# One queue per slot parity in the weight staging, one semaphore per staging slot, and matmuls that wait for layer-norm chunks one by one

## What is computed

```python
def layer(x, W_r, W_i, lambd, W_fc, ln_w, ln_b, W_proj):      # x: 16 x 2048 x 1024
    u = layernorm(x)                                          # over the 1024 features
    r = sigmoid(u @ W_r.T); i = sigmoid(u @ W_i.T)
    log_a = 8.0 * r * log_sigmoid(lambd)
    a = exp(log_a); b = sqrt(max(1 - exp(2 * log_a), 0)) * (i * u)
    h[t] = a[t] * h[t-1] + b[t]                               # scan over time
    x = x + h
    v = gelu(layernorm(x) @ ternary(W_fc).T)                  # 4096 features
    return x + layernorm(v, ln_w, ln_b) @ ternary(W_proj).T
# ternary(W): sign(W) * min(round(|W| / mean|W|), 1)
```

## Time and profile before

| what | us |
|---|---|
| timed runs, two | 2238.38 and 2451.46 |
| their median | 2344.92 |
| the profiled execution, its own time | 2241.78 |
| its span on core 2, the slowest | 2240.2 |
| spans of the other cores | 2213.9 to 2233.6 |
| PE busy, of the span | 1478.6 (66%) |
| DVE busy | 1017.4 (45%) |
| ACT busy | 619.1 (28%) |
| POOL busy | 312.0 (14%) |

### The profile page before, as it was taken

How to read it: one execution, slowest core, us unless ns; L and a number is a source line. 1 busy time by engine, 2 the same in 40 slices (tenths; PEclk the granted TensorE clock), 3 DMA queues, 4 the chain that set the end, 5 groups by cost and what they waited for, 6 DMA issues and landing times.

```text
span 2240.2 us, 20128 instructions; the slowest of 8 cores (2213.9 to 2240.2 us)
## 1 busy us (share of the span) xinstructions
PE 1478.6 (66%) x6052; PEld 610.7 (27%) x6052; DVE 1017.4 (45%) x1457; ACT 619.1 (28%) x1013; POOL 312.0 (14%) x308
## 2 busy tenths in 40 slices
PE   0045104765868867795959595959497777858697
PEld 0012001221323323341424142423242333323243
DVE  0144655663553255425642565145623553256413
ACT  0038332110432234122423132214221332224220
POOL 0122122531120021101110111011100110011100
PEclk9978556986888979796969697979797888979799
DMA  4546797852312122211320231113021312122114
GB/s 123 140 150 230 220 295 235 192 142 75 106 45 104 48 72 79 103 48 38 113 103 10 66 122 38 66 47 123 29 104 47 95 57 104 48 66 85 66 31 129
DMA packets 103745, 223.67 MB, mean 100 GB/s; under 512 B 34516, under 2 KB 34516, under 8 KB 103640
## 3 DMA queue, kind: packets, MB, share of 16 engines
q1 hardware_dynamic: 91352, 178.34, 25.4%
q0 software_dynamic: 12288, 44.05, 6.8%
HBM read 192.98 MB, written 29.37 MB: 99 GB/s over the span
## 4 chain that ended last, share of the span: by engine, by line
PE 58%; DVE 17%; DMA 12%; issue 6%; ACT 6%; DVEq 0%; POOL 0%; SPq 0%; ACTq 0%; POOLq 0%
PE pY L498 21%; PE pool L782 19%; PE pool L631 5%; PE pool L642 3%; PE pS L768 2%; DMA xb<-wit 2%; PE pQ L770 2%; DVE tmp L601 2%; DVE ln_bf L603 2%; DVE tmp L283 2%; DMA xb<-wfct 2%; DVE ln_bf L285 2%; PE pS L472 2%; DMA wp_sc<-qn_buf 2%; DMA t_i<-wpt 2%
## 5 line engine op out<-in xcount | busy, mean ns | idle before, releaser
L782 PE MATMUL pool<-ln_bf,wfc_q 128*128 128x512 bf16 x2048 | 506.8, 394 | 100.3 <-DVE ln_bf L285 100.3
L498 PE MATMUL pY<-g_sb,wp_sl 128*128 128x512 bf16 x2048 | 467.5, 389 | 57.4 <-DVE tmp L520 41.1
L782 PEld LDWEIGHTS pool<-ln_bf,wfc_q 128*128 128x128 bf16 x2048 | 206.0, 101 | 371.2 <-issue 146.8
L498 PEld LDWEIGHTS pY<-g_sb,wp_sl 128*128 128x128 bf16 x2048 | 203.7, 100 | 314.7 <-issue 85.1
L790 ACT ACTIVATE g_sb<-pool 128x512 bf16<-128x512 f32 x256 | 152.6, 597 | 445.0 <-PE pool L782 444.9
L797 DVE TENSOR_TENSOR gsq<-g_sb 128x512 bf16<-128x512 bf16 x224 | 95.4, 426 | 389.9 <-ACT g_sb L790 377.5
L631 PE MATMUL pool<-ln_bf,wr_sl 128*128 128x512 bf16 x512 | 141.2, 425 | 113.8 <-DVE ln_bf L603 113.8
L666 ACT ACTIVATE t_r<-pool 128x512 f32<-128x512 f32 x64 | 37.9, 592 | 374.7 <-PE pool L631 374.7
L601 POOL TENSOR_TENSOR t_r<-xb,rs_t 128x512 f32<-128x512 f32 x16 | 25.6, 1600 | 760.7 <-DVE mb_t L482 759.6
L642 PE MATMUL pool<-ln_bf,wi_sl 128*128 128x512 bf16 x512 | 125.8, 390 | 0.0
L689 DVE SCALAR_TENSOR_TENSOR t_q<-t_a 128x512 f32<-128x512 f32 x64 | 44.2, 691 | 176.6 <-ACT t_a L677 176.6
(11 more groups left out here) (119 smaller groups left out, 1677.2 us busy)
## 6 DMA issues: line engine op xcount, KB each, us to landing
wp_sl<-wp_sc SPq DMA_DIRECT2D x128, 512.0 KB, 4.1
xb<-x SPq DMA_DIRECT2D x8, 2048.0 KB, 9.1
wr_sl<-wr_sc SPq DMA_DIRECT2D x64, 256.0 KB, 2.7
wi_sl<-wi_sc SPq DMA_DIRECT2D x64, 256.0 KB, 2.9
xb<-wfct SPq DMA_DIRECT2D x32, 512.0 KB, 7.0
xb<-wfct POOLq DMA_DIRECT2D x32, 512.0 KB, 6.9
y<-xb SPq DMA_DIRECT2D x8, 2048.0 KB, 7.8
t_q<-wpt POOLq DMA_DIRECT2D x16, 512.0 KB, 5.3
```

Of the source, the lines that this page charges most:

```text
L498: fn = lambda E, kh=kh, sl=sl, bank=bank, first=(kh == 0), last=last: E.matmul(pY[bank][:, :], wp_sl[:, sl * 2048 + (kh % 16) * 128: sl * ...
L782: fn = lambda E, h=h, d=d, bank=bank: E.matmul(pool[bank][:, :], wfc_q[:, d * H + h * 128: d * H + h * 128 + 128], lnch(d), start=(d == 0) ...
```

## The change

Four things are changed. Line numbers of the new code are not given; names are the same.

1. Staging: all eight pieces of W_r come first, then those of W_i, and the slot of `qn_buf` now has the parity of `kd`. So load and scatter of a piece stand on the same queue. The loads of the rearranged slices wait for the last scatter of each of the four slots.
2. The pass over both big weights: `iload` is gone, each piece's two loads stand in the piece's own turn, and the W_proj load counts on the semaphore of the W_fc load of its slot (`d_stg0` to `d_stg3`).
3. The second pass over W_proj uses the same four semaphores; `d_stg4` and `d_stg5` no longer exist.
4. Products with `ln_bf` (both gates and FC1) take the chunks in the order `DPERM`, each with a wait for its own chunk. Line 708 on VectorE waits for chunk `e` alone.

```diff
+DPERM = (0, 1, 6, 2, 3, 7, 4, 5)
...
-    tok_wsc = {}
-    for kd in range(ND):
-        for widx, (WSRC, WSC) in enumerate(((WRT, wr_sc), (WIT, wi_sc))):
-            slot = (kd * 2 + widx) % 4
+    for widx, (WSRC, WSC) in enumerate(((WRT, wr_sc), (WIT, wi_sc))):
+        for kd in range(ND):
+            slot = (widx * ND + kd) % 4
...
-            tok_wsc[(widx, kd)] = emit_scatter(slot, dst, src2)
+            emit_scatter(slot, dst, src2)
+    tok_wrsc = list(sc_last.values())
+    tok_wisc = []
...
-        iload(0)
-        iload(1)
         for i in range(32):
...
-            iload(i + 2)
-            tl = fcq_tl.pop(i)
-            tl2 = gp_tl.pop(i)
+            usewait(qeng, ("stg", sl))
+            tl = b.emit(qeng, lambda E, st=st, kd=kd, pc=pc:
+                        E.dma_start(st, WFCT[128 * kd:128 * (kd + 1), 1024 * pc:1024 * (pc + 1)]),
+                        inc=f"d_stg{sl}", n=16)
...
+            tl2 = b.emit(qeng2, lambda E, st2=st2, i=i:
+                         E.dma_start(st2, WPT[128 * i:128 * (i + 1), :]), inc=f"d_stg{sl}", n=16)
...
-                              E.dma_start(st, WPT[128 * i:128 * (i + 1), :]), inc=f"d_stg{4 + sl % 2}", n=16)
+                              E.dma_start(st, WPT[128 * i:128 * (i + 1), :]), inc=f"d_stg{sl}", n=16)
...
-            b.wait("tensor", tok_ln1)
-            b.wait("tensor", tok_ln1g)
...
-            for d in range(ND):
-                fn = lambda E, d=d, sl=sl, pR=pR: E.matmul(
+            for ii, d in enumerate(DPERM):
+                b.wait("tensor", ln1lt[d])
+                fn = lambda E, d=d, sl=sl, pR=pR, ii=ii: E.matmul(
                     pR[:, :], wr_sl[:, sl * D + d * 128: sl * D + d * 128 + 128], lnch(d),
-                    start=(d == 0), stop=(d == ND - 1))
+                    start=(ii == 0), stop=(ii == ND - 1))
...
-            b.wait("vector", tok_ln1)
-            b.wait("vector", tok_ln1g)
+            b.wait("vector", ln1lt[e])
...
-        b.wait("tensor", tok_ln2[0])
-        b.wait("tensor", tok_ln2[1])
...
-            for d in range(ND):
-                fn = lambda E, h=h, d=d, bank=bank: E.matmul(
+            for ii, d in enumerate(DPERM):
+                b.wait("tensor", tok_ln2[d])
+                fn = lambda E, h=h, d=d, bank=bank, ii=ii: E.matmul(
```

More of the change, by code:

```diff
@@ L323, in emit_prep2a_mid @@
             st = xstg[sl]
-            st2 = tstg[sl]
-            iload(i + 2)
-            tl = fcq_tl.pop(i)
-            tl2 = gp_tl.pop(i)
+            qeng = "sync" if sl % 2 == 0 else "gpsimd"
+            usewait(qeng, ("stg", sl))
+            tl = b.emit(qeng, lambda E, st=st, kd=kd, pc=pc:
+                        E.dma_start(st, WFCT[128 * kd:128 * (kd + 1), 1024 * pc:1024 * (pc + 1)]),
+                        inc=f"d_stg{sl}", n=16)
+            st2 = tstg[sl]
+            qeng2 = "sync" if sl % 2 == 0 else "gpsimd"
+            if i < 4:
+                usewait(qeng2, (tkeymap[sl], 0))
+                usewait(qeng2, (tkeymap[sl], 1))
+            else:
+                usewait(qeng2, ("tstg", sl))
+            tl2 = b.emit(qeng2, lambda E, st2=st2, i=i:
+                         E.dma_start(st2, WPT[128 * i:128 * (i + 1), :]), inc=f"d_stg{sl}", n=16)
             b.wait("vector", tl)
@@ L355, in emit_prep2a_mid @@
         tok_x[1] = b.emit("sync", lambda E, d=dst1, s=src1: E.dma_start(d, s), inc="d_x1", n=16)
-        return (ln2_toks[5], ln2_toks[7])
+        return [ln2_toks[c] for c in range(ND)]
     p2b_loads = {}
@@ L531, in emit_wri_load @@
         usewait("sync", ("wrsl", sl))
-        for kd2 in range(ND):
-            b.wait("sync", tok_wsc[(0, kd2)])
+        for t_ in tok_wrsc:
+            b.wait("sync", t_)
         tok_wr[(k, e, 0)] = b.emit("sync", lambda E, e=e, sl=sl:
@@ L536, in emit_wri_load @@
         usewait("sync", ("wisl", sl))
-        for kd2 in range(ND):
-            b.wait("sync", tok_wsc[(1, kd2)])
+        for t_ in tok_wisc:
+            b.wait("sync", t_)
         tok_wr[(k, e, 1)] = b.emit("sync", lambda E, e=e, sl=sl:
@@ L591, in emit_ln1 @@
         pr = tok_ln2_of.get(k - 1)
-        tok_bc1 = rows_and_bcast(tstat1, 2, rs_t, mb_t, prev_read=pr[0] if pr else None,
-                                 prev_read_g=pr[1] if pr else None)
+        tok_bc1 = rows_and_bcast(tstat1, 2, rs_t, mb_t, prev_read=pr[5] if pr else None,
+                                 prev_read_g=pr[7] if pr else None)
         lt = []
@@ L605, in emit_ln1 @@
             lt.append(tln)
-        tok_ln1_of[k] = (lt[5], lt[7])
+        tok_ln1_of[k] = lt
         free.pop(("lnbf",), None)
@@ L613, in build_nc @@
         seq, t0 = k // 4, (k % 4) * T
-        tok_ln1, tok_ln1g = tok_ln1_of[k]
+        ln1lt = tok_ln1_of[k]
+        tok_ln1, tok_ln1g = ln1lt[5], ln1lt[7]
         for e in (0, 1):
@@ L640, in build_nc @@
             usewait("tensor", ("pool", 2 * q + 1))
-            for d in range(ND):
-                fn = lambda E, d=d, sl=sl, pI=pI: E.matmul(
+            for ii, d in enumerate(DPERM):
+                fn = lambda E, d=d, sl=sl, pI=pI, ii=ii: E.matmul(
                     pI[:, :], wi_sl[:, sl * D + d * 128: sl * D + d * 128 + 128], lnch(d),
-                    start=(d == 0), stop=(d == ND - 1))
-                if d == ND - 1:
+                    start=(ii == 0), stop=(ii == ND - 1))
+                if ii == ND - 1:
                     tok_i = b.emit("tensor", fn, inc="pe")
@@ L733, in build_nc @@
                   for c in range(ND)]
-            tok_ln2 = (lt[5], lt[7])
+            tok_ln2 = lt
         tok_ln2_of[k] = tok_ln2
```

24 lines of the change are left out of this document (2 added, 22 removed).

## The result

| | before | after |
|---|---|---|
| timed, median us | 2238.89 (10 runs) | 2191.1 (11 runs) |
| ratio after / before | | 0.9801, 95% interval 0.9775 to 0.9828 |
| profiled execution: its own time | 2241.78 | 2188.82 |
| span of the slowest core | 2240.2 (core 2) | 2187.2 (core 1) |
| median of the eight spans | 2229.6 | 2182.4 |

The forecast was 2190, and 2191.1 came. The gain is 2.0%, its interval lies on both sides of the 2% that the forecast took as its bound. Some executions were disturbed (one die at a lower clock); ratios leave them out.

The account below looks back on a forecast made before the run. TensorE's waits were taken to count in full in blocks 1 to 7, serial loads at the start, bytes in the big pass. From 2241.8 us, -27 + 4 - 1 - 16 - 10.5 - 1.5 = -52 gave 2190, range 2160 to 2222.

Parts of the forecast that it names:

- Part 1: Staging of W_r and W_i: each queue keeps its own pieces, last cast at 85.7 us, 27 us less.
- I take 7.2, between the two: Staging: assumed load landing time in us, between 7.9 (double step) and 6.1 (median), giving a period of 9.6.
- Part 2: Pass over W_fc and W_proj in block 0: W_proj loads wait for their piece's W_fc load, 4 us more.
- the other queue fills that while engines are at 96%: Big pass: when one queue runs almost dry at a landing, the other keeps the DMA engines busy; +4 us.
- 106 to 112 us long at 90% or more: Sign expected for the big pass in block 0: its length and its DMA share.
- Part 3: Second W_proj pass: the load for slot 2 no longer waits for that of slot 0, 1 us less.
- Part 4: Matmuls after both layer norms, chunk by chunk: one product left after the last chunk; blocks 1 to 7, -16 and -10.5.
- Block 0: Chunk-by-chunk products in block 0: layer norm 1 gains about 1.5 us, layer norm 2 nothing.
- The clock: Rival: products strewn between chunks raise TensorE's clock by the last chunk; 20 us more gained, 2170; chance 0.18.
- Shared engines: Rival: in staging two loads share the DMA engines, period 12.5, last cast at 106, only 6 us saved, 2211; chance 0.13.
- dry pass: Rival: the big pass runs dry and costs its bound of 29 us, 2215; chance 0.08.
- Slower: Rival: in the big pass a queue never has two loads in flight, 14.3 us a pair, 2304; chance 0.04.

Follow-up runs that it names:

- e1: The kernel before with only the new staging of W_r and W_i: 2218.53 us, ratio 0.9885.
- e11: The kernel before with only the staging slot's parity changed, W_r and W_i pieces still alternating: 2229.63 us, ratio 0.9928.
- e12: Like e11, but W_r and W_i alternate by pairs of pieces, so VectorE casts for the two queues in turn; ratio to the kernel before 0.9837, 2209.73 us.
- e2: The kernel before with only the changes to both weight passes (no look-ahead, W_proj loads on the W_fc load's semaphore): 2258.89 us, ratio 1.0046.
- e4: The changed kernel with W_proj loads of both passes again on an own semaphore for each queue: 2183.38 us, ratio 0.972 to the kernel before.
- e3: The kernel before with only the chunk-by-chunk matmuls: 2211.48 us, ratio 0.9855.
- e7: The changed kernel with an own semaphore for each of the four W_proj slots: 2176.03 us, ratio 0.9714 to the kernel before.
- e6: The changed kernel with four gate-weight staging slots and loads issued two pieces ahead on each queue: 2178.8 us, ratio 0.9745 to the kernel before.

## Why the prediction was right, and where its terms were off

- **Part 1, -27.** Measured -29.7 in the changed kernel and -27.7 alone (e1). The mechanism was right but half told: the forecast spoke of the DMA queues crossing, and e11 and e12 show that most of it, 18 of 28 us, was VectorE's order of the casts. The period came out at 8.0 us, below the stated bound of 8.45, while the first two casts ended 2.4 us later than the 18.5 of the forecast (20.9). Loads landed after 5.7 us at the median on the slowest core, not 7.2; on the median of the cores it is 5.4, against 5.2 before. The step that was off is "I take 7.2, between the two": the one double step that it leaned on, 7.9 us with both loads started together, was slower than the pairs that run 1.3 us apart now. Two loads were not in flight throughout, as its sign had it, but 1.3 on the mean.
- **Part 2, +4.** The term that was mis-sized: +14.1, and +16.3 alone (e2), inside the stated bounds of 0 and 29. The step that failed is "the other queue fills that while engines are at 96%". The 96% was the share of one window with 4.4 loads in flight on the mean of that core, of which the change leaves 3.1; it can't vouch for the state after. Over the whole pass the share was 0.91 and fell to 0.80. So the sign "106 to 112 us long at 90% or more" did not come true. e4 shows that it is the semaphore, as the forecast had it, and not the look-ahead.
- **Part 3, -1.** Nothing that shows (e2: 158.9 against 158.6).
- **Part 4.** Layer norm 1: forecast 2.3 us a block. The stretch from its broadcast product to that of layer norm 2 fell from 114.9 to 112.7, on the mean over eight cores and blocks 1 to 7: 2.2. Line 669 waits for the second gate as worked out. Layer norm 2: forecast 1.5; the stretch from its broadcast to the output products fell from 90.0 to 88.1: 1.9. On the slowest cores the output products of one block start 232.1 us after those of the block before, in place of 236.1 (mean of six). Seven times 4 is 28 of the 30.5 us; most of the rest lies in block 1, which became 5.3 shorter. The forecast of 1.5 supposed that the clock's rise keeps its moment. It did not quite: on the mean it came 4.7 us after the last chunk of layer norm 2 before, and 4.1 after it now. In both traces a rise 1 us later goes with a stretch 0.5 us longer, so the earlier rise is worth an estimated 0.3 of the 1.9, and the products 1.6, as forecast. Block 0: e3 alone has 134.2 us in place of 134.4 in the stage with its gates, so the 1.5 there is not shown.
- **Rivals.** The clock did not rise during the layer norm: in block 1 it is still 0.50 from 655 to 656 us, 2 us after the product behind the last chunk, and on no core and in none of the blocks 1 to 7 did it rise sooner than 2.8 us after the last chunk of either layer norm. Only the moment behind it moved, as said. Shared engines, dry pass: the last cast is far from 106, and the pass is 14, not 29, longer. Slower: the pair time on SP is 7.5, not 10.3.
- **The sum.** -52 against -47.2 on the median span and -53 on the slowest core. That 2190 was met so closely is in part luck: part 1, block 0's gates and part 4 gained 7 us more than forecast, the big pass and what follows it lost 12 more.

## What to carry to other kernels

The staging's DMA engines were half idle (0.51), and what shortened it was more loads in flight. In such a stage count the loads in flight and look for the wait that limits them, in the queues and also in the in-order list of the engine that consumes them. A semaphore that two streams share is a wait between them (here 10.6 us of a pass of 117); give each slot of each stream its own. A busy share that was reached with a certain number of transfers in flight says nothing about a change that lowers that number. And starting a product group chunk by chunk behind its producer leaves only the products that stand behind the last chunk: here that was worth 1.6 us before each FC1, and the clock's earlier rise an estimated 0.3 more.

## What was not expected

In the big pass latency and throughput went opposite ways each time:

| the big pass | loads in flight (median of 8 cores) | W_fc landing, us (slowest core) | length, us (median of 8 cores) |
|---|---|---|---|
| changed kernel | 3.0 | 6.1 | 117.3 |
| e4, two semaphores more | 4.3 | 7.9 | 106.7 |
| e7, four semaphores more | 6.2 | 10.2 | 101.7 |

The landing time alone would have ranked them backwards. (In the staging e6 shows the same, 8.2 us to landing and a shorter stage; part 1 does not, where the landing hardly moved.) And reordering 16 casts on VectorE, an engine that was busy some 12 of 112 us, without touching either DMA list, took 18 us off the start (e11 to e12).
